# One attention-and-experts kernel on one core: the order of TensorE's work within a turn, the value product split by block, and tile norms made jobs of their own

## What is computed

```python
for i in range(16):                       # heads, one after another
    att = einsum('btd,bsd->bts', q_rot, k_rot) * scale
    if cascade_bias is not None:
        att = att + cascade_w[i - 1] * cascade_bias   # from head i - 1
    att = softmax(where(causal, -inf, att), axis=-1)
    out_i = einsum('bts,bsd->btd', att, v[:, i])
    cascade_bias = mean(att, axis=1, keepdims=True)   # mean over the queries
x = layernorm(x + concat(out) @ Wproj)
logits = x @ gate_w.T                     # one of 8 experts for each token
out = out + u * silu(g) @ w_down[e].T     # u, g from xs = x * sigmoid(top)
x = layernorm(x + out)
```

## Time and profile before

| | |
|---|---|
| median of three runs | 3801.25 us |
| the profiled execution | 3807.39 us, its span 3805.5 us |
| TensorE busy (matmul) | 3177.0 us, 83% |
| TensorE weight loads | 1694.9 us, 45% |
| VectorE busy | 2628.4 us, 69% |
| ScalarE busy | 3128.9 us, 82% |
| GpSimd busy | 2037.0 us, 54% |
| mean granted clock of TensorE | 0.967 of full speed |
| turns: first to last row maximum of an a0 | 81.6 to 3530.6 us |

### The profile page before, as it was taken

How to read it: one execution, slowest core, us unless ns; L and a number is a source line. 1 busy time by engine, 2 the same in 40 slices (tenths; PEclk the granted TensorE clock), 3 DMA queues, 4 the chain that set the end, 5 groups by cost and what they waited for, 6 DMA issues and landing times. The chain is left out here.

```text
span 3805.5 us, 86407 instructions
## 1 busy us (share of the span) xinstructions
PE 3177.0 (83%) x26666; PEld 1694.9 (45%) x26666; DVE 2628.4 (69%) x7948; ACT 3128.9 (82%) x8911; POOL 2037.0 (54%) x6216
## 2 busy tenths in 40 slices
PE   5788888888888888888888888888888888878755
PEld 3344344434444344444444444444444444444544
DVE  6566566666777777777776777777777776777656
ACT  3799999998888988888788898888778898888524
POOL 5455455554554356665554556665555534454337
PEclk8899999999999999999999999999999999999977
DMA  4333323233433343443443434445334323443455
GB/s 155 89 69 67 78 65 66 64 80 73 102 97 88 87 113 94 120 112 95 99 106 96 105 77 109 110 113 124 94 93 104 95 59 86 97 108 88 122 153 165
DMA packets 223455, 372.37 MB, mean 98 GB/s; under 512 B 50261, under 2 KB 165725, under 8 KB 210896
## 3 DMA queue, kind: packets, MB, share of 16 engines
q1 hardware_dynamic: 206544, 324.77, 34.8%
q0 software_dynamic: 15360, 37.87, 3.9%
q10 hardware_dynamic: 1088, 4.19, 0.3%
HBM read 261.86 MB, written 104.92 MB: 96 GB/s over the span
## 5 line engine op out<-in xcount | busy, mean ns | idle before, releaser
L987 DVE CUSTOM_DVE_ANT_0 att_a<-scores,window 128x128 f32<-128x128 f32 (+7 forms) x2048 | 1493.2, 756 | 687.9 <-PE scores L654 560.7
L848 ACT ACTIVATE att_a<-att_a,neg_max 128x128 f32<-128x128 f32 (+7 forms) x2048 | 1580.6, 772 | 337.8 <-DVE neg_max L987 330.8
L860 ACT ACTIVATE att_t<-scores 128x1024 f32<-128x1024 f32 (+7 forms) x2048 | 1313.0, 641 | 112.7 <-PE scores L673 104.2
L671 PE MATMUL scores<-q_stack,k_stack 104*128 104x512 bf16 (+3 forms) x3072 | 808.3, 333 | 375.8 <-DVE neg_max L987 208.0
L697 PE MATMUL pv<-att_t,v_sb 128*32 128x128 f32 (+1 forms) x13312 | 877.3, 324 | 46.5 <-DVE o_sb L1021 35.8
L1309 POOL TENSOR_SCALAR guess<-row_sum 128x8 f32<-128x8 int32 x256 | 52.8, 206 | 1267.4 <-ACT att_a L848 1266.2
L654 PE MATMUL scores<-k_stack,q_stack 99*128 99x512 bf16 (+3 forms) x3072 | 685.5, 332 | 22.1 <-DVE att_t L1034 10.1
L697 PEld LDWEIGHTS pv<-att_t,v_sb 128*32 128x32 f32 x13312 | 466.6, 109 | 469.4 <-issue 217.2
L671 PEld LDWEIGHTS scores<-q_stack,k_stack 104*128 104x128 bf16 x3072 | 241.6, 98 | 843.6 <-DVE neg_max L987 574.2
L673 PE MATMUL scores<-identb,mask 128*128 128x128 bf16 x2048 | 454.5, 222 | 0.0
L860 ACT ACTIVATION_READ_ACCUMULATOR att_t<-scores 128x1 f32 x2048 | 406.5, 198 | 0.0
(11 more groups left out here) (359 smaller groups left out, 4328.0 us busy)
## 6 DMA issues: line engine op xcount, KB each, us to landing
runner_r<-in_experts SPq DMA_DIRECT2D x140, 384.0 KB, 4.1
qk_parts<-parts SPq DMA_DIRECT2D x128, 384.0 KB, 3.0
q_stack<-qk_parts SPq DMA_DIRECT2D x378, 128.0 KB
k_stack<-qk_parts SPq DMA_DIRECT2D x378, 128.0 KB
xT<-in_xt SPq DMA_DIRECT2D x28, 1024.0 KB, 6.0
head_out<-o_sb SPq DMA_DIRECT2D x252, 64.0 KB
x_rows<-finisher_f SPq DMA_DIRECT2D x28, 514.0 KB, 4.2
finisher_f<-head_out SPq DMA_DIRECT2D x56, 256.0 KB, 4.5
```

The costliest lines, as they stand in the source:

```text
L671: engine.matmul(scores[:, c0:c1], ks[0:ROWS_B, j * P:(j + 1) * P], qs[0:ROWS_B, j * P + c0 - base:j * P + c1 - base], start=True, stop=True)
L848: engine.activation(taken, taken, EXP, scale=-1.0, bias=neg_max[:, n, i:i + 1], accum_out=row_sum[:, n, i:i + 1]).then_inc(s_exp_a, 1)
L860: engine.activation(att_t[:, ring:ring + end - base], scores[:, base:end], EXP, accum_out=col_sum[:, n, j:j + 1]).then_inc(s_exp_b, 1)
L987: engine.tensor_tensor_reduce(out=att_a[:, ring:ring + end - base], in0=scores[:, base:end], in1=window[:, T - (end - base):T], op0=ALU.ad ...
```

## The change

TensorE's program of a turn becomes: a0 a1 b1 b2, v6, side | a2 a3, v7, two sides | b3 b4, v0 | a4, rows, a5, v1, side | b5 b6, v2 v3 | a6 a7, side | b7, v4 v5, side | b0 of the next turn, two sides. The number of side stages that a step takes is now given by a table, 1, 2, 0, 1, 0, 1, 1, 2, eight per turn as before. The rows' transpose stands behind a4, and VectorE's copy of them behind a4's row maximum. A value block now waits for its own exponential only. The batch norms become jobs of their own, which begin when the batch's last statistics are placed; the runner's next tile goes on meanwhile, held back only in that its `t_down` is placed at least LAG (5) steps after the last `t_out` of the batch before. `TILES` is 39.

```diff
-    TILES = GBLK + E
+    TILES = GBLK + E - 1
...
-    def tile_job(g, r):
+    def tile_jobs(g, r):
...
+        norms = []
...
+            out_before = (("t_out", (g, tiles[m - m % BATCH - 1]), LAG),) if m >= BATCH else ()
...
-                    Stage("t_down", n, 2, hold=2), Stage("t_add", n, 1, frees=True), Stage("t_stat", n, 1)]
+                    Stage("t_down", n, 2, hold=2, after=out_before), Stage("t_add", n, 1, frees=True), Stage("t_stat", n, 1)]
...
-                b = (g, tuple(tiles[m - q:m + 1]))
-                job += [Stage("t_aggr", b, 1), Stage("t_root", b, 2, phase=GPSIMD), Stage("t_newton", b, LAG), Stage("t_norm", b, 1)]
-                job += [Stage("t_out", (g, j_), 2 if j_ == tiles[m - q] else 0, phase=GPSIMD) for j_ in tiles[m - q:m + 1]]
-        return job
+                of = tiles[m - q:m + 1]
+                b = (g, tuple(of))
+                norms.append([Stage("t_aggr", b, 0, after=(("t_stat", n, 1),)), Stage("t_root", b, 2, phase=GPSIMD),
+                              Stage("t_newton", b, LAG), Stage("t_norm", b, 1)]
+                             + [Stage("t_out", (g, j_), 2 if j_ == of[0] else 0, phase=GPSIMD) for j_ in of])
+        return [job] + norms
...
+    PE_PLACES = (1,2,0,1,0,1,1,2)
...
-            pe_free = True
+            pe_free = PE_PLACES[i] if inside else 1
...
-                    if s.kind in PE_KINDS:
-                        pe_free = False
+                    if s.kind in PE_KINDS and inside:
+                        pe_free -= 1
...
-        VALUE_ORDER = {2: (2, 0), 4: (2, 2), 6: (2, 4), 0: (3, 6)}
+
+        VALUE_ORDER = {0: [(3, 6)], 1: [(3, 7)], 2: [(2, 0)], 3: [(2, 1)], 4: [(2, 2), (2, 3)], 5: [], 6: [(2, 4), (2, 5)], 7: []}
...
-                pe.wait_ge(s_exp_b, k + 2 - k % 2)
+                pe.wait_ge(s_exp_b, k + 1)
...
-                    for which, block in FILL_ORDER[i]:
+                    for n, (which, block) in enumerate(FILL_ORDER[i]):
...
+                        for stage in st.stages:
+                            if stage.kind == "rows" and n == 0:
...
-                    if i in VALUE_ORDER:
-                        behind, j = VALUE_ORDER[i]
+                    for behind, j in VALUE_ORDER[i]:
                         if 0 <= x_ - behind < UNITS:
                             att_v(x_ - behind, j)
-                            att_v(x_ - behind, j + 1)
...
-                    for stage in st.stages:
-                        if stage.kind == "rows":
-                            copy_rows(x_, stage)
-                    for block in TAKE_ORDER[i]:
+                    for n, block in enumerate(TAKE_ORDER[i]):
                         if x_ < UNITS:
                             row_max(x_, block)
+                        for stage in st.stages:
+                            if stage.kind == "rows" and n == 0:
+                                copy_rows(x_, stage)
```

More of the change, by code:

```diff
@@ L213, in tile_job @@
                     Stage("t_up", n, 0, frees=True),
-                    Stage("t_down", n, 2, hold=2), Stage("t_add", n, 1, frees=True), Stage("t_stat", n, 1)]
+                    Stage("t_down", n, 2, hold=2, after=out_before), Stage("t_add", n, 1, frees=True), Stage("t_stat", n, 1)]
             q = m % BATCH
             if q == BATCH - 1 or m == len(tiles) - 1:
-                b = (g, tuple(tiles[m - q:m + 1]))
-                job += [Stage("t_aggr", b, 1), Stage("t_root", b, 2, phase=GPSIMD), Stage("t_newton", b, LAG), Stage("t_norm", b, 1)]
-                job += [Stage("t_out", (g, j_), 2 if j_ == tiles[m - q] else 0, phase=GPSIMD) for j_ in tiles[m - q:m + 1]]
-        return job
+                of = tiles[m - q:m + 1]
[4 more added lines that the diff above has]
+        return [job] + norms
     PE_KINDS = {"qk_a", "qk_b", "v_a", "v_b", "f_pa", "f_pb", "f_t", "f_gate", "f_turn", "r_count", "r_sum", "t_turn", "t_gu",
                 "t_down"}
+    PE_PLACES = (1,2,0,1,0,1,1,2)
     def timetable():
-        steps, placed, active = [], set(), []
+        steps, placed, active = [], {}, []
         banks = {n: 0 for n in range(2)}
@@ L230, in timetable, with not_yet @@
         turned = True
+        def not_yet(a, t):
+            kind, key, gap = a if len(a) == 3 else a + (0,)
+            if isinstance(key, int) and key < 0:
+                return False
+            return (kind, key) not in placed or t < placed[kind, key] + gap
         def step(x_, i):
@@ L254, in step @@
                         break
-                    if any(a[1] >= 0 and a not in placed for a in s.after):
+                    if any(not_yet(a, t) for a in s.after):
                         break
@@ L347, in timetable @@
                         del waiting["route", g]
-                        waiting["tiles", g] = [begin(tile_job(g, r_)) for r_ in range(RUN[g])]
+                        waiting["tiles", g] = [begin(job) for r_ in range(RUN[g]) for job in tile_jobs(g, r_)]
         g = GROUPS - 1
@@ L360, in timetable @@
         for r_ in range(RUN[g]):
-            begin(tile_job(g, r_))
+            for job in tile_jobs(g, r_):
+                begin(job)
         while active:
@@ L719, in tensor_program @@
                             fill_b(x_ + 1, block)
-                    if i in VALUE_ORDER:
-                        behind, j = VALUE_ORDER[i]
+                        for stage in st.stages:
+                            if stage.kind == "rows" and n == 0:
+                                if x_ - 1 < UNITS:
+                                    pe.wait_ge(s_shifted, x_)
+                                if x_ >= 3:
+                                    pe.wait_ge(s_biased, biased_count(x_ - 3))
+                                wait_bank(pe, stage.before)
+                                engine.transpose(bank_ap(stage.bank)[0:TURNED, 0:P // 2].bitcast(BF16), bits[:, :],
+                                                 identb[:, :]).then_inc(s_rows, 1)
+                    for behind, j in VALUE_ORDER[i]:
                         if 0 <= x_ - behind < UNITS:
                             att_v(x_ - behind, j)
-                            att_v(x_ - behind, j + 1)
                 for stage in st.stages:
```

4 lines of the change are left out of this document (1 added, 3 removed).

## The result

The changed kernel takes 3746.07 us (median of four runs, 3743.6 to 3750.12); the kernel before, beside it, 3802.56 us. The ratio is 0.9847 with a 95% interval of 0.982 to 0.9873: 1.5% faster. The forecast was 3698 us; some 56 us were gained where 103 were forecast. The time lies inside the stated range, 3605 to 3795. The profiled execution took 3743.6 us.

The account below looks back on a forecast made before the run. No engine is full; ScalarE's exponentials set light turns and TensorE's side work stretches others. Terms -205 + 107 - 5 + 5 - 5 = -103 us take the profiled 3807.4 to 3704, 3698 on the median's scale; range 3605 to 3795.

Parts of the forecast that it names:

- signs of being right: Idle before a4 under 60 us, a6 under 30; a4's maximum not behind rows; 78 tail DMAs; light turns near 11.8 us.
- signs of being wrong: Idle before b 256 or a 128 over 100 us, or b5's fill waited for; tile turns still 14.4 us; t_add waiting.
- Fills that come earlier: ScalarE's idle time before a4, a6 and a2 in the turns falls: -205 us together, bounds -262 and -100.
- Side stages that go elsewhere: Stages moved from steps 2 and 4 to 1 and 7, 214 us of TensorE, cost +107 us; bounds 0 and 214.
- Tiles: In the turns, three fewer tiles give -5 us; norms as own jobs cost +5, bounds 0 and +25.
- Tail: Last group's tiles after the turns, bound by GpSimd's issue: -5 us, bounds -13 and +8.
- TensorE has room: Rival: moved side stages cost nothing, falling in waits of b2, b5 and b7; about 3600 us, chance 0.15.
- doubled places stall ScalarE: Rival: 3850 us, chance 0.12; sign: idle before b3 and a0 grows more than a4, a6 and a2 lose.
- No net effect: Rival: gains and costs cancel, within 0.2% of 3801 us; chance 0.05.
- TensorE is the bound in loaded turns: Rival: earlier fills only move the wait, only lightly loaded turns gain, -35 us in the turns; 3760 us, chance 0.2.
- the second term: The +107 us for side stages moved to steps 1 and 7, priced at 0.5 us per us of TensorE moved.

Follow-up runs that it names:

- joined kernel: The changed kernel with value blocks v0 v1 together again in step 2 and v6 v7 in step 0; 0.9692 of the kernel before.
- pl_e: The joined kernel with step 7's second side stage put back in step 4, ahead of a6; 0.9771 of the kernel before.
- pl_b: The joined kernel with step 1's second side stage put back in step 2, ahead of a4; 0.9807 of the kernel before.

## Why the prediction came out as it did

The direction was right and the range held the time; the size was about half of the forecast. The four signs of being right are there: 27.5 us ahead of a4 and 8.3 ahead of a6, a4's row maximum no longer behind the rows' transpose, 78 indirect DMAs from the first gather on, 11.6 us for a light turn. But so are two of the signs of being wrong: ScalarE waits for b5's fill, and t_add waits for the scatter.

- *Fills that come earlier*: forecast -205 us of ScalarE's idle time, measured -213 (a4 -128 for -115, a6 -77 for -70, a2 -8 for -20). Right.
- *Side stages that go elsewhere*: forecast +107 for new waits. Measured in the first profile: b5 +73, b3 +37, b0 +23, a0 +4, 137 in all, and 25 more at the copy of v. In the joined kernel the same four stand 92 us above before (b5 +36, b3 +13, b0 +40, a0 +4) and the copy of v is back at 29.0, though that trace is of the slower setting. So for the moved stages and the rows alone, 107 was about right. Which waits would grow was only in part foreseen: b5 was called next late, but a us earlier than before, and it became the largest new wait.
- **The step that failed** stands in the part on the fills: a4 "loses from ahead of it v1", priced at 0.2 us, and a2 "gains v7", priced at 0.4, as if a block could be moved at its share of the pair. Behind a4 v1 was again counted at 0.2 us; alone it takes 0.34. No term stood for breaking a group of matmuls in two. It costs 0.27 us of TensorE a turn in the timeline, some 70 us over the turns. And what a4 and a2 gained by it is small: 11 and 12 us of ScalarE's wait, against 71 lost at b5 and b3 (changed kernel against joined). Joining the pairs gained 1.3%, some 47 us, as much as is missing. How much of that is the cost of the break and how much the later place of v1 and v7 is not shown.
- The Trainium skill (Perfetto Trace Analysis, Identifying the Most-Contended Engine) says that the busy share of matmuls is no good measure of how near a kernel is to its limit, and names the busy share of weight loads as one of two better ones. In this case the weight loads alone would have misled: with the pairs split they are busy for less time, 1457 us against 1534, the matmuls for more, 3041 against 2937, and the kernel is slower.
- The Trainium skill (TensorE: Matmul & The Clock Gate, Part 3: Packing small matmuls, on row and column tiling) states that small matmuls placed in different tiles of the array run at the same time. The trace agrees: v7's four matmuls, one for each of four column groups, take 0.35 us, and v1's single one, in one column group, takes 0.34. So v1 alone leaves most of the array unused. But that does not explain the whole cost: breaking v6 v7, where v7 alone has all four column groups, costs as much (0.57 + 0.35 against 0.79) as breaking v0 v1 (0.57 + 0.34 against 0.77). Some cost comes with each separate start of a value block; what it is was not tried.
- *Tiles*: forecast 0 in the turns, with a bound of +25; the tile part costs 15 us of the turns in the new order.
- *Tail*: forecast -5, measured +3.5: -7.6 in the tiles themselves, +11 ahead of them. The t_add that waits for a late scatter, named as a bound, is there. Why the stretch ahead of the tiles grew is not settled; other tables make it 147 and 158 us (pl_e, pl_b), so it hangs on how the planner spreads the jobs.
- *The rivals*. That TensorE has room (the moved stages cost nothing) falls: new waits of 137 us, and 92 even with the pairs joined. That the doubled places stall ScalarE falls by its own sign: b3 and a0 grew by 41 us, a4, a6 and a2 shrank by 213. No net effect falls. "TensorE is the bound in loaded turns" came nearest in the number, 3760, but not in the mechanism: a4's and a6's waits did go, and a good part of what came back was work and order that the change itself added.
- *Luck*: the 0.5 per us in the second term was a choice without a row behind it, and it came out right. The forecast's own range, 3640 to 3755, held the time only just, and nothing in it stood for the split.

## What to carry to other kernels

When a stream is cut to let an urgent instruction pass, price the cut: time the pieces apart and together, and let the urgent one pass only as far as it still needs. Put filler work by how long its neighbour on the other engine is busy, not one piece to each step; here that table, with hardly anything else, matched the whole change. And look at what a placement does to the backlog: of the variants of the joined kernel the one with the shortest turns (3336.9 us) was no faster than the others, because the work it left undone stood behind them.

## What the runs showed of the hardware that was not expected

Two fp32 instructions of v1, 128 columns into one quarter of the array, hold TensorE for 0.34 us alone, about as long as v7's eight into all four quarters (0.35), and add only 0.2 us to v0's eight, which take 0.57 alone and 0.77 with them.

The same kernels ran 1.2 to 1.4% slower in one setting than in another (kernel before 3858 and 3861 against 3807 us). For the changed kernel 27 of the 43 us are in the turns (3407.7 against 3380.7) and 17 behind them (295.2 against 278.4), though the granted clock of the turns is 0.98 in both. The exponentials take the same time to 1 or 2 ns in the mean, and 182 of 255 turns are the same to 0.1 us. What differs are waits here and there that no instruction in the profile ends, marked "remote". ScalarE has 22 to 46 us of them in each of the eight traces of the slower setting, and none in the six of the faster one. The largest group of the changed kernel, in the faster setting and in the slower one:

```profile
L875 ACT ACTIVATE att_t<-scores 128x640 f32<-128x640 f32 x256 | 179.1, 700 | 1.3 <-PE pv L714 0.9
```

```profile
L875 ACT ACTIVATE att_t<-scores 128x640 f32<-128x640 f32 x256 | 179.1, 700 | 12.7 <-remote 7.1 <-PE pv L714 5.1
```

What causes them is open, and how much of the difference they make too.
